# VectorE's reciprocals two tiles later and its division one tile later in the heads of a softmax attention

## Chip, cores and metric

One core of a Trainium2 chip runs one launch of the whole kernel. The metric is the device time in microseconds (us), lower is better. TensorE (PE) multiplies matrices, VectorE (DVE), ScalarE (ACT) and GpSimd (POOL) work on elements, and SyncE (SP) issues the transfers (DMA).

## What is computed

A block with a modulated layernorm, 16-head attention over 1024 tokens with a position bias, a gated residual, and then two layers of windowed attention with an MLP. The change lies in the first attention, for 2 batches x 16 heads = 32 heads:

```python
attn = jnp.einsum('bhqd,bhkd->bhqk', q, k) / math.sqrt(HD)
attn = attn + slopes[None, :, None, None] * rel[None, None, :, :]
attn = jax.nn.softmax(attn, axis=-1)
out = jnp.einsum('bhqk,bhkd->bhqd', attn, v)
```

## The kernel before

The kernel is written with one instruction stream for each engine and semaphores between them. The stage of the change is a loop over heads i = 0 to 31, and in each over tiles k = 0 to 7 of 128 keys (or, for the maxima, of 128 queries). Three heads are in work at a time:

- **Maxima of head i + 2.** TensorE writes a tile of raw scores (`max_step`, L836) into PSUM banks 4 and 5. VectorE adds the bias and takes the maximum of each row (`max_step`, L765: one long instruction and a short one that writes `M`). From head 2 on all tiles use the same two banks, so TensorE's scores of tile k + 1 wait until VectorE has written the maximum of tile k (`max_done`, L833). The eight maxima are turned by TensorE in the next head (`turn_m`, L842).
- **Scores, exponentials and products of head i.** TensorE writes scores with the maxima taken off (`qk_step`, L862), ScalarE takes exponentials into one of four buffers `E` (L738), TensorE multiplies them with the values (`pv_step`, L872). VectorE adds the exponentials of tiles 3, 5 and 7 (`sum_step`, L775: 3 + 5 behind the maximum of tile 5, and + 7 as the first thing of the next head), GpSimd those of the others and VectorE's sum (L684, L688).
- **Denominators and division of head i - 1.** In tile 2, TensorE sums GpSimd's result over partitions (`denominators`, L881), ScalarE copies it (`take_denominators`, L715), VectorE takes reciprocals in two halves (`invert`, L782), SyncE writes them to DRAM and reads them back spread over the partitions by two transfers (`spread_inverse`, L645 and L649), and VectorE multiplies the head's product by them (`divide`, L790, two instructions).

TensorE's order within a pair of tiles k, k + 1 (k even) is: scores k and k + 1, the maximum's scores of tile k, value products of tiles k - 1 and k, behind them in tile 2 the denominators and `turn_m`, then the maximum's scores of tile k + 1. Its value products of tile 0 of head i + 1 wait for the division of head i - 1 (L870), because they write the same bank.

SyncE's order in a head is: in every fourth head the keys and values of the next group (`load_kv`), queries (`load_qa`), the row of maxima (`load_m`), then `spread_inverse`.

In what follows "max 3" is the maximum of tile 3, on either engine as said. In the trace `XF` is the name under which the reciprocals and denominators stand, `xpos_sb` that of the sums, `junk` that of the maxima's discarded output.

Of the kernel before, what the change touches and what calls it, by code (L numbers as in the profile page):

```python
# [76 lines left out]
def need(eng, sem, count):  # L77

    if count > 0:
        eng.wait_ge(sem, count)  # L80
# [11 lines left out]
def adaln_block(nc, x, wq, wk, wv, wo, f_wqkv, f_qs, f_ks, f_wo, f_lg, f_lb, f_w1, f_b1, f_w2, f_b2,  # L92
# [7 lines left out]
    with ExitStack() as whole:  # L100
# [14 lines left out]
        def banks(a, n=1):  # L115
            return psum[:, a:a + n, :].rearrange("p b c -> p (b c)")
# [53 lines left out]
        with ExitStack() as ph:  # L170
# [63 lines left out]
            def need_landed(eng, b):  # L234

                for s in range(2):
                    eng.wait_ge(t_out[b][s], 48 * (TB // 2))
                    eng.wait_ge(v_out[b][s], 16 * (TB // 2))
# [308 lines left out]
        def residual(dve, t):  # L547

            s = t % 2
            need(dve, proj_done, t // 4 * 4 + 4 if t < TB else t + 1)  # L550
            dve.tensor_tensor(y[:, s, :], projected(t), rows[:, t // TB, ga, :], ALU.mult).then_inc(res_step, 1)
            dve.wait_ge(res_step, 4 * t + 1)
            dve.tensor_tensor(X[:, t, :], X[:, t, :], y[:, s, :], ALU.add).then_inc(res_step, 1)
            dve.wait_ge(res_step, 4 * t + 2)
            dve.bn_stats(bn[:, s, :], X[:, t, :]).then_inc(res_step, 1)
            dve.wait_ge(res_step, 4 * t + 3)
            dve.bn_aggr(mv[:, t, :], bn[:, s, :]).then_inc(res_step, 1)
# [22 lines left out]
        with ExitStack() as ph:  # L580
# [40 lines left out]
            def max_bank(i, k):  # L621

                return 4 if i >= 2 else (4, 0, 2)[(TB * i + k) % 3]
# [7 lines left out]
            with nc.Block() as block:  # L631
# [124 lines left out]
                @block.vector  # L756
                def _(dve):
                    def max_step(i, s, k):

                        need(dve, max_mm, TB * i + k + 1)  # L760
                        if k == 0:
                            need(dve, alibi_done, i + 1)
                            need(dve, m_turned, i - 1)
                        need(dve, max_done, TB * i + k)
                        dve.tensor_tensor_reduce(junk[:, :], banks(max_bank(i, k), 2), alibi[:, s, :], -1.0, BIG, ALU.add, ALU.min,  # L765
                                                 M[:, s, k:k + 1]).then_inc(max_done, 1)

                    def sum_step(i, s, n):
                        k = DVE_SUMS[n + 1]
                        need(dve, exp_done, TB * i + k + 1)  # L770
                        need(dve, sum_d_done, ND * i + n)
                        if n == 0:
                            need(dve, sum_p_done, NP * (i - 1))
                        first = E[:, DVE_SUMS[0] % 4, :] if n == 0 else sum_d[:, s, :]
                        dve.tensor_tensor(sum_d[:, s, :], first, E[:, k % 4, :], ALU.add).then_inc(sum_d_done, 1)  # L775

                    def invert(i, half):

                        need(dve, den_taken, i + 1)
                        need(dve, inv_out, 16 * i)  # L780
                        part = slice(half * DQ // 2, (half + 1) * DQ // 2)
                        dve.reciprocal(den_inv[:, part], den_sb[:, part]).then_inc(inv_done, 1)  # L782

                    def divide(i, ch):

                        need(dve, inv_in, 32 * (i + 1))
                        need(dve, pv_done, TB * (i + 1))
                        a, r = HD * ch, HD * (i % 2)
                        dst = OT[r:r + HD, i // H, (i % H) // 2, 4 * ch:4 * ch + 4, :].rearrange("p t c -> p (t c)")
                        dve.tensor_tensor(dst, banks(6 + i % 2)[a:a + HD, :], inv_wide[a:a + HD, :], ALU.mult)\  # L790
                            .then_inc(o_done, 1)

                    def head(i):
                        for k in range(TB):
                            if k == 0 and i > 0:
                                sum_step(i - 1, (i - 1) % 2, 1)
                            if i + 2 < HEADS:
                                max_step(i + 2, i % 2, k)
                            if k in (2, 3) and i > 0:
                                invert(i - 1, k - 2)  # L800
                            if k == 5:
                                sum_step(i, i % 2, 0)
                            if k == 6 and i > 0:
                                for ch in range(2):
                                    divide(i - 1, ch)

                    for i in range(2):
                        for k in range(TB):
                            max_step(i, i, k)
                    need_landed(dve, 1)  # L810
                    for i in range(HEADS):
                        head(i)
                    sum_step(HEADS - 1, (HEADS - 1) % 2, 1)

                    for half in range(2):
                        invert(HEADS - 1, half)
                    for t in range(EARLY):
                        residual(dve, t)
                    for ch in range(2):
                        divide(HEADS - 1, ch)  # L820
# [739 lines left out]
```

## Time and profile before

| | before |
|---|---|
| median of 3 runs | 1317.8 us (1313.16 to 1318.82) |
| the profiled execution's own time | 1316.46 us |
| its span, first to last instruction | 1314.7 us |
| TensorE busy in the span | 1115.1 us (85%) |
| VectorE busy | 1049.2 us (80%) |
| GpSimd busy | 849.0 us (65%) |
| ScalarE busy | 735.6 us (56%) |
| TensorE's granted clock, mean | 0.943 |

Busy time is the time in which an engine had an instruction in work; the span is a little shorter than the execution's own time, which has the start and end of the launch in it. The stage with the 32 heads lies between about 165 us and 800 us.

### The profile page before, as it was taken

The page shows a single profiled execution, that of the slowest core. Times are in us where ns is not written, and L with a number is a line of the kernel's source. Part 1 is how long each engine was busy: PE and PEld are TensorE (multiplying, and loading weights), DVE is VectorE, ACT ScalarE, POOL GpSimd, SP SyncE. Part 2 cuts the span into 40 slices and gives each one's busy share as a digit, 9 for nine tenths or more (in the row PEclk, how much of TensorE's full clock was granted, in tenths as well). Part 3 has the DMA queues.
Part 4 walks back from the last instruction along what each step waited for, and adds up shares of the span by engine and source line. Part 5 has one row for each costly group of instructions (what it writes and reads, how often), then busy time and mean ns, then how long its engine had stood idle before and what let it go on. Part 6 is the DMA issues. An engine that isn't in the chain of part 4 may idle for free. (4 is left out here: it accounts for less than half of the span.)

```text
span 1314.7 us, 23737 instructions
## 1 busy us (share of the span) xinstructions
PE 1115.1 (85%) x8256; PEld 692.6 (53%) x8256; DVE 1049.2 (80%) x2026; ACT 735.6 (56%) x1512; POOL 849.0 (65%) x488
## 2 busy tenths in 40 slices
PE   5776579999999999999999999467777896778788
PEld 3554535544455454555445548234555684455578
DVE  6898577777777777777777746599999589999957
ACT  3666625555555555555555551257676755777664
POOL 4556216566566666656656664698789249999916
PEclk9888769999999999999999999789898997999899
DMA  7567932142413314241331001000111100111111
GB/s 230 136 173 198 283 80 57 42 97 65 105 42 86 76 42 97 65 105 38 83 83 52 23 17 56 34 17 19 27 28 28 31 3 8 27 28 29 30 31 33
DMA packets 95237, 88.91 MB, mean 68 GB/s; under 512 B 22884, under 2 KB 74768, under 8 KB 95120
## 3 DMA queue, kind: packets, MB, share of 16 engines
q1 hardware_dynamic: 95120, 87.41, 26.2%
q8 instruction: 66, 1.08, 0.3%
q14 instruction: 51, 0.42, 0.1%
HBM read 53.57 MB, written 24.25 MB: 59 GB/s over the span
## 5 line engine op out<-in xcount | busy, mean ns | idle before, releaser
L738 ACT ACTIVATE E<-psum,keybias_sb 128x1024 f32<-128x1024 f32 x256 | 274.8, 1112 | 249.1 <-PE psum L862 235.9
L765 DVE CUSTOM_DVE_ANT_0 junk<-psum,alibi 128x1024 bf16<-128x1024 f32 x256 | 309.4, 1209 | 93.0 <-PE psum L836 80.2
L684 POOL TENSOR_TENSOR xpos_sb<-xpos_sb,E 128x1024 f32<-128x1024 f32 x96 | 231.2, 2408 | 130.7 <-ACT E L738 126.2
L872 PE MATMUL psum<-E,V 128*64 128x512 f32 x1024 | 248.0, 605 | 0.0
L836 PE MATMUL psum<-KH,QH 64*128 64x512 f32 x512 | 124.7, 481 | 20.9 <-DVE M L765 16.7
L688 POOL TENSOR_TENSOR xpos_sb<-xpos_sb 128x1024 f32<-128x1024 f32 x32 | 76.1, 2377 | 90.7 <-DVE xpos_sb L775 90.7
L1195 ACT ACTIVATE E_att<-S_att,nmax_att 128x128 f32<-128x128 f32 x256 | 99.0, 389 | 43.7 <-DVE nmax_att L1229 43.6
L1142 POOL TENSOR_TENSOR rinv_att<-ss_up_att,minus_half 128x16 f32<-128x16 f32 x32 | 120.8, 3775 | 2.7
L872 PEld LDWEIGHTS psum<-E,V 128*64 128x64 f32 x1024 | 62.1, 136 | 112.7 <-issue 105.7
L836 PEld LDWEIGHTS psum<-KH,QH 64*128 64x128 f32 x512 | 50.6, 191 | 124.1 <-DVE M L765 92.6
L782 DVE RECIPROCAL XF<-XF 128x128 f32<-128x128 f32 x64 | 60.4, 948 | 64.1 <-ACT XF L715 64.1
L862 PE MATMUL psum<-QH,KH 64*128 64x512 f32 x512 | 106.4, 406 | 3.4 <-ACT XF L715 1.0
L862 PE MATMUL psum<-QL,KH 64*128 64x512 f32 x512 | 103.4, 392 | 0.0
L862 PE MATMUL psum<-QH,KL 64*128 64x512 f32 x512 | 103.1, 391 | 0.0
L862 PE MATMUL psum<-QM,one_rows 64*128 64x512 f32 x512 | 103.0, 390 | 0.0
L1132 POOL TENSOR_TENSOR t_att<-raw_att,xpos_sb 128x1024 f32<-128x1024 f32 x32 | 100.5, 3142 | 0.0
L1323 PE MATMUL psum<-kT_att,qT_att 64*64 64x128 f32 x1024 | 42.4, 310 | 66.3 <-DVE nmax_att L1229 66.1
L684 POOL TENSOR_TENSOR xpos_sb<-E 128x1024 f32<-128x1024 f32 x32 | 76.4, 2388 | 30.0 <-ACT E L738 24.8
L1248 DVE TENSOR_TENSOR qk_att<-qk_att,rinv_att 128x1024 f32<-128x1024 f32 x32 | 90.3, 2823 | 5.8 <-POOL rinv_att L1142 4.7
L1323 PEld LDWEIGHTS psum<-kT_att,qT_att 64*64 64x64 f32 x1024 | 33.9, 152 | 88.6 <-issue 88.0
L1127 POOL TENSOR_TENSOR sq_att<-raw_att 128x1024 f32<-128x1024 f32 x32 | 66.6, 2083 | 14.1 <-ACT raw_att L1202 14.1
L1313 PE MATMUL psum<-fw_qkv,hT_att 128*128 128x512 f32 x128 | 66.1, 642 | 2.1 <-ACT raw_att L1202 2.1
(145 smaller groups left out, 2399.9 us busy)
## 6 DMA issues: line engine op xcount, KB each, us to landing
qa_scratch<-tT SPq DMA_DIRECT2D x32, 512.0 KB, 4.1
QH<-qa_scratch SPq DMA_DIRECT2D x64, 256.0 KB, 4.2
QL<-qa_scratch SPq DMA_DIRECT2D x64, 128.0 KB, 4.2
XF<-inverse_scratch SPq DMA_DIRECT2D x64, 128.0 KB, 2.9
vp_att<-v_att SPq DMA_DIRECT2D x64, 128.0 KB, 2.3
k_scratch<-tT SPq DMA_DIRECT2D x16, 256.0 KB, 4.6
KH<-k_scratch SPq DMA_DIRECT2D x16, 256.0 KB, 3.9
KL<-k_scratch SPq DMA_DIRECT2D x16, 256.0 KB, 5.1
```

The source lines that it names most:

```text
L684: pool.tensor_tensor(sum_p[:, s, :], first, E[:, k % 4, :], ALU.add)\
L688: pool.tensor_tensor(sum_p[:, s, :], sum_p[:, s, :], sum_d[:, s, :], ALU.add)\
L738: act.activation(E[:, k % 4, :], scores(k % 2), ACT.Exp, bias=kb).then_inc(exp_done, 1)
L765: dve.tensor_tensor_reduce(junk[:, :], banks(max_bank(i, k), 2), alibi[:, s, :], -1.0, BIG, ALU.add, ALU.min, M[:, s, k:k + 1]).then_inc(m ...
L836: last = pe.matmul(banks(max_bank(i, k) + ch), QH[rows, s, k * P:(k + 1) * P], KH[rows, g, ch * 512:(ch + 1) * 512], start=True, stop=True)
L862: last = pe.matmul(scores(k % 2)[:, ch * 512:(ch + 1) * 512], key[rows], query[rows, a:a + 512], start=(n == 0), stop=(n == len(terms) - 1))
L872: last = pe.matmul(banks(6 + i % 2)[HD * ch:HD * ch + HD, :], V[:, g, k, :], E[:, k % 4, ch * 512:(ch + 1) * 512], start=(k == 0), stop=(k ...
L1132: pool.tensor_tensor(t2[:, s].rearrange("p (q h) d -> p q h d", q=2), raw[:, s].rearrange("p (q h) d -> p q h d", q=2), sin, ALU.mult)\
L1142: pool.tensor_tensor(rinv[:, s, :], ss_up[:, s, :], minus_half[:, 0:NH], ALU.pow)\
L1195: act.activation(E[:, s, h, :], S[:, s, h, :], ACT.Exp, bias=nmax[:, s, h:h + 1], scale=-1.0, accum_out=den[:, s, h:h + 1]).then_inc(exp_d ...
L1248: dve.tensor_tensor(qk[:, s], qk[:, s], rinv[:, s, :][:, :, None].to_broadcast([P, NH, HD]), ALU.mult).then_inc(qk_done, 1)
L1323: last = pe.matmul(banks(5 + h % 2)[WIN * w:WIN * w + WIN, (h // 2) * P:(h // 2 + 1) * P], qT[a:a + HD, s, h // 2, WIN * w:WIN * w + WIN], ...
```

## The change

In heads with i > 0 VectorE's two reciprocals move from behind max 2 and max 3 to behind max 4 and max 5, and the division from behind max 6 to behind max 7. Nothing else is edited.

```diff
                             if i + 2 < HEADS:
                                 max_step(i + 2, i % 2, k)
-                            if k in (2, 3) and i > 0:
-                                invert(i - 1, k - 2)
+                            if k in (4, 5) and i > 0:
+                                invert(i - 1, k - 4)
                             if k == 5:
                                 sum_step(i, i % 2, 0)
-                            if k == 6 and i > 0:
+                            if k == 7 and i > 0:
                                 for ch in range(2):
                                     divide(i - 1, ch)
```

VectorE's row before, in head 1, from max 2 to the sum behind max 5 (each maximum is a row with `junk,M` and one with `M`):

```order
L765 ISA junk,M<-psum,alibi 128x1024
L765 ISA M 128x1
L782 RECIPROCAL XF<-XF 128x128
L765 ISA junk,M<-psum,alibi 128x1024
L765 ISA M 128x1
L782 RECIPROCAL XF<-XF 128x128
L765 ISA junk,M<-psum,alibi 128x1024
L765 ISA M 128x1
L765 ISA junk,M<-psum,alibi 128x1024
L765 ISA M 128x1
L775 TENSOR_TENSOR xpos_sb<-E 128x1024
```

The same stretch of the changed kernel, again from max 2 to the sum behind max 5:

```order
L765 ISA junk,M<-psum,alibi 128x1024
L765 ISA M 128x1
L765 ISA junk,M<-psum,alibi 128x1024
L765 ISA M 128x1
L765 ISA junk,M<-psum,alibi 128x1024
L765 ISA M 128x1
L782 RECIPROCAL XF<-XF 128x128
L765 ISA junk,M<-psum,alibi 128x1024
L765 ISA M 128x1
L782 RECIPROCAL XF<-XF 128x128
L775 TENSOR_TENSOR xpos_sb<-E 128x1024
```

The reciprocals now stand behind max 4 and max 5, and the second one is followed at once by the sum. Directly behind comes the second place, which before reads from max 6 through max 7 to max 0 of the next head:

```order
L765 ISA junk,M<-psum,alibi 128x1024
L765 ISA M 128x1
L790 TENSOR_TENSOR OT<-psum,XF 64x512 x2
L765 ISA junk,M<-psum,alibi 128x1024
L765 ISA M 128x1
L775 TENSOR_TENSOR xpos_sb<-xpos_sb,E 128x1024
L765 ISA junk,M<-psum,alibi 128x1024
L765 ISA M 128x1
```

And in the changed kernel it reads, from the same max 6 to the same max 0:

```order
L765 ISA junk,M<-psum,alibi 128x1024
L765 ISA M 128x1
L765 ISA junk,M<-psum,alibi 128x1024
L765 ISA M 128x1
L790 TENSOR_TENSOR OT<-psum,XF 64x512 x2
L775 TENSOR_TENSOR xpos_sb<-xpos_sb,E 128x1024
L765 ISA junk,M<-psum,alibi 128x1024
L765 ISA M 128x1
```

The division moved behind max 7 and is followed at once by the sum with which the next head begins. The rows of TensorE, ScalarE, GpSimd and SyncE are the same in both kernels. In heads 30 and 31 no maxima are left, and there VectorE's row is the same in both kernels too.

## Rows read from the trace of the kernel before

**Rows 1.** Busy time by stretch: start:end, length, busy (instructions) per engine, clock, DMA share, GB/s

```profile
212.65:751.37 538.72, 527.80 (x3392) 270.07 (x3389) 414.87 (x616) 284.44 (x308) 335.86 (x141) 1.00 0.28 69
...
164.00:175.00 11.00, 6.63 (x20) 2.40 (x16) 9.45 (x15) 2.67 (x5) 0.20 (x1) 0.50 0.20 55
```

**Rows 2.** Waits between 212.65 and 751.37 us: total, times, longest

```profile
PE psum L836 <- DVE M L765: 8.5, 15, 1.6
DVE OT L790 <- DMA XF<-inverse_scratch: 6.0, 7, 1.4
```

**Rows 3.** Timeline of TensorE, one head: start us, duration us, engine, line, what

```profile
521.87 0.51 PE L836 MATMUL psum<-KH,QH 64*128 64x512 f32 x2
...
524.35 0.47 PE L836 MATMUL psum<-KH,QH 64*128 64x512 f32 x2
...
526.61 0.50 PE L836 MATMUL psum<-KH,QH 64*128 64x512 f32 x2
...
530.97 0.51 PE L836 MATMUL psum<-KH,QH 64*128 64x512 f32 x2
...
532.71 0.40 PE L862 MATMUL psum<-QH,KL 64*128 64x512 f32 x2
532.94 0.39 PE L862 MATMUL psum<-QM,one_rows 64*128 64x512 f32 x2
533.39 0.49 PE L836 MATMUL psum<-KH,QH 64*128 64x512 f32 x2
...
535.69 0.50 PE L836 MATMUL psum<-KH,QH 64*128 64x512 f32 x2
...
540.82 0.50 PE L836 MATMUL psum<-KH,QH 64*128 64x512 f32 x2
```

**Rows 4.** Timeline of VectorE, the same head

```profile
522.22 0.95 DVE L782 RECIPROCAL XF<-XF 128x128 f32<-128x128 f32 x1 [1.64 <-ACT XF L715]
523.09 1.16 DVE L765 CUSTOM_DVE_ANT_0 junk<-psum,alibi 128x1024 bf16<-128x1024 f32 x1
...
524.18 0.95 DVE L782 RECIPROCAL XF<-XF 128x128 f32<-128x128 f32 x1
...
527.15 1.22 DVE L765 CUSTOM_DVE_ANT_0 junk<-psum,alibi 128x1024 bf16<-128x1024 f32 x1 [0.94 <-PE psum L836]
...
528.30 1.22 DVE L775 TENSOR_TENSOR xpos_sb<-E 128x1024 f32<-128x1024 f32 x1
529.44 1.22 DVE L765 CUSTOM_DVE_ANT_0 junk<-psum,alibi 128x1024 bf16<-128x1024 f32 x1
...
530.58 1.40 DVE L790 TENSOR_TENSOR OT<-psum,XF 64x512 f32<-64x512 f32 x2
532.01 1.23 DVE L765 CUSTOM_DVE_ANT_0 junk<-psum,alibi 128x1024 bf16<-128x1024 f32 x1
533.16 0.08 DVE L765 DVE_READ_ACCUMULATOR2_ANT M<- 128x1 f32 x1
```

**Rows 5.** Timeline of SyncE's transfer issues, the same head

```profile
525.15 0.51 SPq L645 DMA_DIRECT2D inverse_scratch<-XF  x1
526.77 1.14 SPq L649 DMA_DIRECT2D XF<-inverse_scratch  x2
```

**Rows 6.** The spreading transfers, all 64: us from issue to landing

```profile
DMA to landing us min/median/max: 2.8/2.9/4.0
```

**Rows 7.** Timeline of SyncE in a head that loads keys and values

```profile
504.64 0.52 SPq L645 DMA_DIRECT2D inverse_scratch<-XF  x1
507.60 1.14 SPq L649 DMA_DIRECT2D XF<-inverse_scratch  x2
```

**Rows 8.** Timeline of VectorE in that head

```profile
511.58 1.41 DVE L790 TENSOR_TENSOR OT<-psum,XF 64x512 f32<-64x512 f32 x2 [1.43 <-DMA XF<-inverse_scratch]
```

**Rows 9.** Timeline of ScalarE, exponentials of tile 7

```profile
529.64 1.11 ACT L738 ACTIVATE E<-psum,keybias_sb 128x1024 f32<-128x1024 f32 x1 [0.44 <-DVE xpos_sb L775]
```

**Rows 10.** Timeline of GpSimd, its last addition of a head

```profile
534.46 2.38 POOL L688 TENSOR_TENSOR xpos_sb<-xpos_sb 128x1024 f32<-128x1024 f32 x1 [2.71 <-DVE xpos_sb L775]
```

## Prediction, written before the changed kernel ran

> **What bounds the kernel now.** I first read the busy time of the stretch with the heads that the change touches, 28 heads from one `turn_m` to that of 28 heads later. TensorE is busy 527.80 of 538.72 us at the full clock, VectorE 414.87 [rows 1]. So the stage goes at TensorE's pace, and one head takes 538.72 / 28 = 19.24 us. The waits of the same stretch come next: TensorE stands 8.5 us for a maximum of VectorE, and VectorE 6.0 us for the spread reciprocals before the division [rows 2]. VectorE has a quarter of its time free, but TensorE can be only one maximum ahead of it, since all use one pair of banks. What decides is therefore where VectorE's extra work stands between two maxima, not how much there is of it.
>
> For that I laid the timelines of one quiet head side by side [rows 3, 4], with time 0 where TensorE starts the scores of max 3 (521.87). TensorE starts those of max 4 at 2.48, max 5 at 4.74, max 7 at 9.10, max 0 of the next head at 11.52, max 1 at 13.82 and the next max 3 at 18.95. The pairs of matmuls ahead of max 0 start 0.23 apart (532.71, 532.94), so it could have started at 533.17, which is 11.30; it did so 0.22 later, 0.15 behind the end of VectorE's max 7 (533.16 + 0.08). Without any wait a head is 18.73 us long. The difference to the mean, 0.51 x 28 = 14.3 us, is all that the best order for VectorE could give back in these heads.
>
> VectorE's durations, start to start so that the overlap of neighbours is counted once, are: a reciprocal 0.87 (522.22 to 523.09), a sum 1.14 (528.30 to 529.44), the division 1.43 (530.58 to 532.01), a maximum 1.15 (532.01 to 533.16), and 1.23 until its result stands. VectorE starts a maximum 0.54 behind TensorE's start (526.61 to 527.15) [rows 3, 4].
>
> **What the change removes.** The first reciprocal waits 1.64 us for ScalarE's copy of the denominators [rows 4]. Behind max 4 the copy has long been made and the wait goes, 28 x 1.64 = 46 us of VectorE. It is worth nothing to TensorE: max 3 comes earlier, but TensorE's max 4 starts at its own pace at 2.48 in either case.
>
> **What it moves, step by step.** Undisturbed, TensorE has 0.54 + 1.23 + 0.15 = 1.92 us of each interval of about 2.2 used up by VectorE, so only about 0.3 is free.
>
> Max 3 starts on VectorE at 0.54, max 4 at 3.02, and VectorE is free at 4.17. The first reciprocal reaches to 5.12, and max 5 would start at 5.28 anyway: it costs nothing. Max 5 leaves VectorE at 6.43. There the second reciprocal (ends 7.38), the sum (starts 7.30) and max 6 (starts 8.44) follow each other. Max 6 stands at 9.67, and TensorE's max 7, due at 9.10, starts at 9.82: **a wait of 0.72 us**.
>
> Max 7 starts on VectorE at 10.36, stands at 11.59, and VectorE is free at 11.51. TensorE's max 0 comes 2.20 behind max 7 (11.30 - 9.10), at 12.02, and waits for nothing. VectorE's max 0 however now has the division and a sum ahead of it. If the division could start at once, max 0 would start at 11.51 + 1.43 + 1.14 = 14.08, stand at 15.31, and TensorE's max 1 would start at 15.46 where 13.60 is due without waits (13.82 less the 0.22). **The order alone thus costs 1.86 us a head**, against the 0.51 of before.
>
> Third, **the division waits**. Between the second reciprocal and the division stood three maxima and a sum of room, now two maxima. The way through DRAM takes, from the end of the reciprocal (524.18 + 0.95), 0.02 to the issue of the write, 1.62 to that of the first read, 0.57 (half of 1.14) to that of the second [rows 5], and 2.9 to its landing [rows 6]: 5.11 us. From 7.38 the landing is at 12.49, and VectorE stands idle for 0.98 us from 11.51. Max 0 then starts at 12.49 + 1.43 + 1.14 = 15.06, stands at 16.29, and TensorE's max 1 starts at 16.44, 2.84 late. The rest, 5.13 us to the next max 3 (535.69 to 540.82 [rows 3]), has only light work for VectorE and is unchanged. A head becomes 18.73 + 2.84 = **21.57 us**, that is 2.33 more than 19.24.
>
> The Trainium skill, DMA: Bandwidth & Descriptors, Anatomy of one DMA, gives each transfer about 2.0 us plus its bytes at 436 GB/s (a fit for another issuing path). By it 4 KB and 128 KB in a row, with the same 0.59 of issues, would make an estimate of 4.9 us in place of 5.11, and the total about 6 us lower; the trace differs in the split (1.62 and 2.9) more than in the sum, and I go by the trace.
>
> What could hide or add to this: TensorE's value products of tile 0 wait for the division, which ends at 13.90; their turn comes at about 12.96 (max 0 and one group of products behind 12.02), but max 1 is later yet at 16.44, so this adds nothing. The exponentials of tile 7, which already waited 0.44 for the sum behind max 5 [rows 9], start at about 8.6 in place of 7.77 and end at 9.8, before the scores that need their bank at about 11. GpSimd's last addition, 2.38 us [rows 10], starts about 15.3 and is done at 17.7, 3 us before the denominators that stand ahead of the next max 3. SyncE issues the queries of a later head right behind the reads, a head before they are needed. The 7 waits of before for the transfers [rows 2] fall mostly in heads that load keys and values; there the write needed 2.96 us until the first read (504.64 to 507.60), and the division came 3.98 behind that [rows 7, 8]. The write now comes four microseconds later in the head, when those loads are through, so I give these heads the ordinary 5.11.
>
> **Sum.** 28 heads x 2.33 = 65.2. At the end of the last head with maxima the wait of 0.72 and the first value products' wait for the division (13.90 + 0.15 - 12.96 = 1.1) add 1.8, less the 0.2 of before: 1.6. Together 66.8 us, on 1316.46: 1383.3. The median of the runs lies 1.3 above that execution, so **1385 us**. The terms for 28 or 29 heads: pile-up before max 7, 20 us; pile-up before max 0 beyond that, 32 us; wait for the transfer, 28 us; less the 14.3 that are lost already.
>
> **Rivals.**
> - *As above, all three terms* (0.72). Its own range is 1372 to 1400: the landing at 2.8 to about 3.4, and some tenths of a microsecond a head on either side.
> - *No wait for the transfer*, only the order costs (0.07). 28 x (20.59 - 19.24) + 0.6 = 38.4, so 1356. For it: with DRAM and queue quiet the chain might be faster. Against: it would have to take 4.1 us from the reciprocal's end, where the fixed parts alone are 2.2 and no read landed under 2.8 [rows 5, 6].
> - *Slow transfers* (0.07). With the longest landing, 4.0 [rows 6], each head is 1.1 longer: 1417. If the chain took everywhere the 6.96 us of the head with loads (0.02 + 2.96 + 3.98 [rows 7, 8]) it would be 1.85 x 29 = 54 more: 1438. For it: the queries' loads now follow the reads at once.
> - *The clock* (0.05). The stage ran at 1.00, but at 0.50, the lower level of 1.2 GHz, where TensorE was busy 6.63 of 11 us before the heads [rows 1]. It will be busy about 18.7 of 21.6. Were the clock low in a tenth of the 600 us, at most half of those 60 us is lost: some 30 us more, 1415.
> - *No change* (0.04). The maxima are for two heads later, and if TensorE's own row let it go on with scores of the current head while VectorE is late, it would lose nothing: 1318. Against: max 1 stands in its row ahead of the next scores, and the 0.22 in the quiet head shows that it does wait.
> - *Faster* (0.05). VectorE's 46 us of waits for the denominators and the 6.0 for the transfers go, and if these were what made the maxima late, up to the 14.3 us come back: 1303. It needs VectorE's maxima 6 and 0 to be on time, so the blocks behind max 5 and max 7 would have to fit in some 0.3 us of room; they are 2.0 and 2.6 us long. It decides only if max 1 starts before 13.8.
>
> **How the numbers follow.** 1385 is the likeliest case. The range, 1364 to 1420, leaves out the cases at 1356, no change and faster (0.16) and the slowest chains, and takes in the bounds of the landing and a partly low clock. A measurement of this kernel can tell about 0.5% from no change. Slower by more than that: 0.72 + 0.07 + 0.07 + 0.05 = 0.91; within it 0.04; faster 0.05.
>
> **What would show it.** In the changed kernel's profile the reciprocals should have no wait for ScalarE, and the division one of about 1 us for the transfer in nearly all of the 29 heads. TensorE's scores of max 7 should start 5.1 us behind those of max 5 (4.4 before), and max 1 about 4.4 behind max 0 (2.3 before); a head should take 21.6 us, with TensorE about 87% busy and a granted clock of 1.00. I am wrong if the division starts right behind max 7, if max 1 isn't late, or if the clock falls.

## The result and the profile after

The changed kernel takes 1414.53 us in the median of 4 runs (1412.35 to 1418.58), before 1317.41 (1313.16 to 1318.82): a ratio of 1.0744, interval 1.0723 to 1.0764, that is 97 us more. The direction came as forecast, and so did the late max 1 and the wait of the division. The time lies in the range of 1364 to 1420, but 30 us above the 1385 that was called likeliest, and the granted clock fell, which the prediction had named as a sign of being wrong. The profiled execution took 1415.14 us, its span 1413.3.

The stretch of the same 28 heads as in [rows 1] comes first, then a run of quiet heads in it and a run of bad ones. The columns are those of [rows 1].

```profile
212.15:847.72 635.57, 551.02 (x3393) 282.39 (x3389) 425.00 (x616) 285.81 (x308) 357.42 (x141) 0.96 0.23 59
347.61:433.88 86.27, 75.66 (x488) 38.24 (x484) 60.72 (x88) 40.65 (x44) 51.10 (x21) 1.00 0.26 65
433.88:558.75 124.87, 105.36 (x610) 54.46 (x606) 75.89 (x110) 51.35 (x55) 65.06 (x26) 0.89 0.25 64
```

A head takes 635.57 / 28 = 22.70 us in place of 19.24. In the four quiet heads it is 86.27 / 4 = 21.57, just as forecast; in the five of the third row 124.87 / 5 = 24.97, with a mean granted clock of 0.89. The waits in the 28 heads, against [rows 2]:

```profile
PE psum L836 <- DVE M L765: 49.6, 56, 1.4
DVE OT L790 <- DMA XF<-inverse_scratch: 40.5, 28, 2.6
PE psum L872 <- DVE OT L790: 33.2, 28, 2.4
```

TensorE's waits for a maximum have gone from 8.5 us in 15 places to 49.6 in 56, two in each head; the division waits for its transfer in every head, 1.45 us in the mean, and TensorE's first value products wait for the division. ScalarE no longer holds up the reciprocals in these heads.

One quiet head on TensorE, which answers to [rows 3]. Max 3 is at 369.32; the following rows are max 7, max 0, one group of value products, the group that waits for the division, max 1 and the next max 3.

```profile
369.32 0.50 PE L836 MATMUL psum<-KH,QH 64*128 64x512 f32 x2
...
378.93 0.50 PE L836 MATMUL psum<-KH,QH 64*128 64x512 f32 x2 [0.45 <-DVE M L765]
381.10 0.40 PE L836 MATMUL psum<-KH,QH 64*128 64x512 f32 x2
381.43 1.08 PE L872 MATMUL psum<-E,V 128*64 128x512 f32 x4
383.32 1.08 PE L872 MATMUL psum<-E,V 128*64 128x512 f32 x4 [0.80 <-DVE OT L790]
385.75 0.50 PE L836 MATMUL psum<-KH,QH 64*128 64x512 f32 x2 [1.35 <-DVE M L765]
...
390.91 0.51 PE L836 MATMUL psum<-KH,QH 64*128 64x512 f32 x2
```

VectorE in the same head, which answers to [rows 4]: the second reciprocal, the sum, max 6, max 7, the division, the other sum and max 0.

```profile
375.71 0.95 DVE L782 RECIPROCAL XF<-XF 128x128 f32<-128x128 f32 x1
376.57 1.16 DVE L775 TENSOR_TENSOR xpos_sb<-E 128x1024 f32<-128x1024 f32 x1
377.65 1.21 DVE L765 CUSTOM_DVE_ANT_0 junk<-psum,alibi 128x1024 bf16<-128x1024 f32 x1
...
379.47 1.23 DVE L765 CUSTOM_DVE_ANT_0 junk<-psum,alibi 128x1024 bf16<-128x1024 f32 x1 [0.60 <-PE psum L836]
...
381.76 1.41 DVE L790 TENSOR_TENSOR OT<-psum,XF 64x512 f32<-64x512 f32 x2 [1.06 <-DMA XF<-inverse_scratch]
383.20 1.23 DVE L775 TENSOR_TENSOR xpos_sb<-xpos_sb,E 128x1024 f32<-128x1024 f32 x1
384.46 1.23 DVE L765 CUSTOM_DVE_ANT_0 junk<-psum,alibi 128x1024 bf16<-128x1024 f32 x1
```

Counted from max 3, the division starts at 12.44 (forecast 12.49), max 1 at 16.43 (16.44), the next max 3 at 21.59 (21.57). The signs that the prediction named are near but not exact: max 7 starts 4.92 us behind max 5 (374.01; forecast 5.1), and max 1 4.65 behind max 0 (4.4). The blocks behind max 5 and max 7 stand as the diff put them, and but for the wait of the division there is no room between their parts.

What the forecast lacks is in other heads. This is TensorE's timeline in one of the bad ones, at the same place: the group that waits for the division, max 1, and two of the eight pairs behind it.

```profile
524.45 1.08 PE L872 MATMUL psum<-E,V 128*64 128x512 f32 x4 [2.37 <-DVE OT L790]
526.88 0.79 PE L836 MATMUL psum<-KH,QH 64*128 64x512 f32 x2 [1.35 <-DVE M L765]
527.47 0.63 PE L862 MATMUL psum<-QH,KH 64*128 64x512 f32 x2
527.89 0.63 PE L862 MATMUL psum<-QL,KH 64*128 64x512 f32 x2
...
530.38 0.40 PE L836 MATMUL psum<-KH,QH 64*128 64x512 f32 x2
```

Two things differ. The wait for the division is 2.37 in place of 0.80 us, since the reciprocals landed later; and the pairs start 0.42 apart where [rows 3] have 0.23, so max 2 comes 3.50 us behind max 1 (2.19 in the quiet head). That is the lower clock of 1.2 GHz: between 527.40 and 529.50 us the granted clock is 0.50. Twelve of the 28 heads have such half-rate pairs behind max 1; five of them, in a row (434 to 558 us), have the long wait as well.

### The profile page after: what moved, and what is told of

It is laid out like the page before. It is cut to its first block and busy times, and to the rows that moved or that the text cites. A ratio compares the mean times of both kernels' runs of the same rounds, so it can differ in the third digit from the quotient of the medians.

```text
span 1413.3 us, 23737 instructions
## 1 busy us (share of the span) xinstructions
PE 1142.1 (81%) x8256; PEld 704.6 (50%) x8256; DVE 1060.0 (75%) x2026; ACT 737.0 (52%) x1512; POOL 871.9 (62%) x488
## 5 line engine op out<-in xcount | busy, mean ns | idle before, releaser
L765 DVE CUSTOM_DVE_ANT_0 junk<-psum,alibi 128x1024 bf16<-128x1024 f32 x256 | 313.2, 1223 | 192.7 <-PE psum L836 180.7
L684 POOL TENSOR_TENSOR xpos_sb<-xpos_sb,E 128x1024 f32<-128x1024 f32 x96 | 254.2, 2647 | 150.4 <-ACT E L738 145.8
L872 PE MATMUL psum<-E,V 128*64 128x512 f32 x1024 | 257.0, 612 | 34.2 <-DVE OT L790 34.2
L862 PE MATMUL psum<-QH,KH 64*128 64x512 f32 x512 | 111.7, 427 | 3.5 <-ACT XF L715 1.0
L862 PE MATMUL psum<-QL,KH 64*128 64x512 f32 x512 | 108.8, 413 | 0.0
L862 PE MATMUL psum<-QH,KL 64*128 64x512 f32 x512 | 108.0, 410 | 0.0
L862 PE MATMUL psum<-QM,one_rows 64*128 64x512 f32 x512 | 107.2, 407 | 0.0
L790 DVE TENSOR_TENSOR OT<-psum,XF 64x512 f32<-64x512 f32 x64 | 44.1, 689 | 44.2 <-DMA XF<-inverse_scratch 43.2
L782 DVE RECIPROCAL XF<-XF 128x128 f32<-128x128 f32 x64 | 60.3, 946 | 15.7 <-ACT XF L715 15.7
```

Source lines behind the costliest of these rows:

```text
L684: pool.tensor_tensor(sum_p[:, s, :], first, E[:, k % 4, :], ALU.add)\
L862: last = pe.matmul(scores(k % 2)[:, ch * 512:(ch + 1) * 512], key[rows], query[rows, a:a + 512], start=(n == 0), stop=(n == len(terms) - 1))
L872: last = pe.matmul(banks(6 + i % 2)[HD * ch:HD * ch + HD, :], V[:, g, k, :], E[:, k % 4, ch * 512:(ch + 1) * 512], start=(k == 0), stop=(k ...
```

## Experiments

Each was timed against the kernel before on the same chip. The period of a head, the waits and the clock are those of the same 28 heads in the profiled execution.

### One part of the change alone

First the reciprocals alone, with the division left behind max 6:

```diff
-                            if k == 7 and i > 0:
+                            if k == 6 and i > 0:
```

> Only the reciprocals are moved (behind max 4 and 5), the division stays behind max 6. Theory (order and transfer): the reciprocals land at 12.5 us of a head's time, so VectorE stands from 9.6 to 12.5 with max 7 queued behind it; max 7 stands at 15.15, TensorE starts max 0 at 15.3 and max 1 at 17.6, 4.0 us late. A head takes 22.7 us, the kernel about 98 us more than before, 1415, and more if the longer gap lowers the clock: ratio 1.075 to 1.10, no better than the whole change. Rival (the division's new place is what costs): it stays where it was, so the time should be within 10 us of before, ratio under 1.01.

Measured: 1475.91 us, ratio 1.121 (1.1177 to 1.1243), above the range of 1.075 to 1.10; a head takes 25.0 us. The rival is refuted: with the division in its old place the loss is larger, not smaller. The division starts where it was forecast, 12.37 us behind max 3 in this head (TensorE's row of max 3 first, then VectorE's division, then TensorE again):

```profile
361.39 0.51 PE L836 MATMUL psum<-KH,QH 64*128 64x512 f32 x2
...
371.00 0.50 PE L836 MATMUL psum<-KH,QH 64*128 64x512 f32 x2 [0.45 <-DVE M L765]
376.58 0.80 PE L836 MATMUL psum<-KH,QH 64*128 64x512 f32 x2 [3.23 <-DVE M L765]
377.31 3.08 PE L872 MATMUL psum<-E,V 128*64 128x512 f32 x8
380.31 0.50 PE L836 MATMUL psum<-KH,QH 64*128 64x512 f32 x2
```

```profile
373.76 1.41 DVE L790 TENSOR_TENSOR OT<-psum,XF 64x512 f32<-64x512 f32 x2 [2.81 <-DMA XF<-inverse_scratch]
```

Max 0 starts at 15.19, forecast 15.30. But I had not priced what follows: behind the gap of 3.23 us the two groups of value products take 3.08 us where 1.94 is usual, and max 1 comes at 18.92 instead of 17.6. The mean clock of these heads is 0.91, and it fell in each of the 28. The division's waits reach up to 4.4 us, but come to 89.1 us in all, 3.2 a head, where my expectation has 2.9. So later landings are worth some 8 of the 60 us above my 1415. The rest lies behind the gap, with the lower clock, and no run took it apart further.

Then the division alone, with the reciprocals left behind max 2 and 3:

```diff
-                            if k in (4, 5) and i > 0:
-                                invert(i - 1, k - 4)
+                            if k in (2, 3) and i > 0:
+                                invert(i - 1, k - 2)
```

> Only the division is moved (behind max 7), the reciprocals stay behind max 2 and 3. Theory: the reciprocals land at about 8.4, the division never waits; with the sum behind it max 0 is late and TensorE starts max 1 at 14.74 in place of 13.60. A head takes 19.9 us in place of 19.24: plus 18 us, 1335, ratio 1.010 to 1.017, clock at 1.00 in the stage. Rival (the division's new place is the cost): most of the 97 us appear here, ratio over 1.04.

Measured: 1338.77 us, ratio 1.0167 (1.014 to 1.0195), a head 19.98 us. The wait of the division is gone and TensorE has one wait of 1.2 to 1.35 us in each head, for max 0, with the clock at 1.00:

```profile
PE psum L836 <- DVE M L765: 35.7, 28, 1.3
```

The two parts do not add up: the first alone costs 160 us, the second 23, both together 97. Moved with the reciprocals, the division's step back lets max 7 pass before the wait for the landing.

### The changed kernel without the transfer

SyncE's `spread_inverse` is left out, with VectorE's wait for the write, and the division waits for one filling of its factors instead:

```diff
-                        if i > 0:
-                            spread_inverse(i - 1, (i - 1) % 2)
...
-                        need(dve, inv_in, 32 * (i + 1))
+                        dve.wait_ge(filled, 4)
```

> The changed kernel without the two-step transfer through DRAM: the division multiplies by constant ones, so the output lacks the softmax denominators; everything else, the reciprocals too, stays. Theory: the wait of the division (1.05 us in ordinary heads, up to 2.6) is gone, the order alone stays: a head takes 20.5 us, 1353, ratio 1.02 to 1.035, and no half-rate matmuls behind max 1. Rival (the order costs all, the transfer nothing): ratio stays near 1.074. Rival (the transfer is all): ratio within 0.5% of 1.

Measured: 1353.29 us, ratio 1.0272 (1.0241 to 1.0304), a head 20.47 us. That is the order's own cost, 37 us; the rest of the 97 hangs on the transfer. The clock stayed at 1.00, although TensorE still waits twice in each head:

```profile
213.13:786.42 573.29, 523.03 (x3393) 268.85 (x3389) 423.73 (x616) 284.30 (x308) 357.17 (x141) 1.00 0.22 52
```

```profile
PE psum L832 <- DVE M L762: 48.6, 56, 1.4
```

(L832 and L762 are the maximum's two lines in this kernel.) What is missing against the changed kernel is the wait for the division between max 0 and max 1.

### The gap filled with work

The changed kernel, with matmuls in the gap that weigh the exponentials with zeros:

```diff
+                        for n in range(extra):
+                            for ch in range(2):
+                                last = pe.matmul(banks(6 + i % 2)[HD * ch:HD * ch + HD, :], zeros[:, :],
+                                                 E[:, k % 4, ch * 512:(ch + 1) * 512], start=False,
+                                                 stop=(n == extra - 1))
                         last.then_inc(pv_done, 1)
```

> The changed kernel, with two more pairs of value products with zero weights behind the last tile of a head, which add nothing to the sums and lie in the gap in which TensorE waits for the division (about 1.9 us of matmuls). Theory (part of the loss is the clock, falling behind the gap of max 0 to max 1): the granted clock of the stage goes from 0.89 to 0.98 to nearly 1.00, no half-rate rows, ordinary heads stay at 21.6 us, and the kernel is some 15 to 20 us faster than the changed one, 1396, ratio 1.055 to 1.063. Rival (the clock's fall lies within the waits and costs nothing): the same 1.074 or slower.

Measured: 1397.58 us, ratio 1.0606 (1.0569 to 1.0644), some 16 us less than the changed kernel by doing more. The profiled execution is the fastest of the four, 1391.94 us; in it a head takes 21.89 us at clock 1.00, and not one of the 28 heads has half-rate pairs. The division waits 38.4 us in all, against 40.5 in the changed kernel, so the gain is not one of earlier landings. In order of time, max 0, the products of tile 7, the added matmuls, the products of tile 0, max 1 and max 2:

```profile
375.93 0.39 PE L837 MATMUL psum<-KH,QH 64*128 64x512 f32 x2
376.25 1.08 PE L876 MATMUL psum<-E,V 128*64 128x512 f32 x4
377.15 1.89 PE L881 MATMUL psum<-E,zeros_m 128*64 128x512 f32 x8
378.87 1.03 PE L876 MATMUL psum<-E,V 128*64 128x512 f32 x4
380.53 0.50 PE L837 MATMUL psum<-KH,QH 64*128 64x512 f32 x2 [0.63 <-DVE M L766]
382.71 0.39 PE L837 MATMUL psum<-KH,QH 64*128 64x512 f32 x2
```

The added 1.9 us of matmuls cost nothing, since TensorE only waits there, and max 2 comes 2.18 behind max 1. The rival, that the low clock hides within the waits, is refuted.

### The queries' loads out of the reads' way

```diff
-                            load_qa(sp, i + 3, (i + 3) % 4)
                         if i + 1 < HEADS:
                             load_m(i + 1, (i + 1) % 2)
+                        if i + 3 < HEADS:
+                            load_qa(sp, i + 3, (i + 3) % 4)
```

> The changed kernel, with SyncE's loads of the queries put behind the row of maxima, so that they are through before the reciprocals are written and do not follow the reads of the reciprocals. Theory (the long waits of 2.2 to 2.6 us in heads 13 to 17 come from the queries' transfers running into the reads): the division waits about 1.0 us in all heads, some 10 us less than the changed kernel, 1402 to 1406. Rival (those long waits are something else): the waits of over 2 us stay, ratio 1.074.

Measured: 1401.43 us, ratio 1.0624 (1.0601 to 1.0647), 13 us less than the changed kernel. (The bad heads that the expectation calls 13 to 17 are heads 11 to 15 of the program.) The division's waits fall from 40.5 to 30.4 us, and one of 28 is above 2 us, where there were five:

```profile
DVE OT L790 <- DMA XF<-inverse_scratch: 30.4, 28, 2.3
```

The waits thus account for 10 of the 13 us; half-rate pairs stand in 10 heads in place of 12. In the changed kernel the loads of the queries, 384 KB twice over, are issued 0.05 us behind the second read, as these rows of SyncE from the quiet head show:

```profile
378.31 1.14 SPq L649 DMA_DIRECT2D XF<-inverse_scratch  x2
379.50 0.59 SPq L157 DMA_DIRECT2D QH<-qa_scratch  x1
```

The intervals of the two kernels lie apart, so the place of the loads costs something. That they are the whole cause of the long waits is not shown: they follow the reads just as closely in the quiet heads (in the head at 369 us and in the bad one at 509), one long wait is left here, and the kernel with the filled gap has four heads in a row with them at another place (646 to 738 us).

### Both together

The last two edits in one kernel should bring back just what the prediction had left out.

> The changed kernel with both edits, the zero-weight products in the gap and the queries' loads behind the row of maxima. Theory (what the changed kernel loses beyond the 2.33 us a head that were predicted is the low clock and the long transfers, and nothing else): no half-rate rows, the division waits about 1.0 us in nearly all heads, every head takes about 21.5 us, the kernel 1382 to 1388, ratio 1.049 to 1.054. Rival (the two effects are one, long waits only making the clock fall): no better than the filled gap alone, ratio 1.060.

Measured: 1387.53 us (1387.06 to 1388.23), ratio 1.0531 (1.0513 to 1.0549), a head 21.65 us:

```profile
212.81:819.09 606.28, 571.97 (x3616) 285.40 (x3613) 424.96 (x616) 284.46 (x308) 357.43 (x141) 1.00 0.25 63
```

Each over its own runs of before, the changed kernel loses 97.1 us, with the gap filled 81.4, with the loads moved 84.1. Gains of 15.7 and 13.0 should leave 68.4; with both it loses 69.0. The intervals of these ratios reach 2 to 5 us to either side, so the agreement to 0.6 us is luck. But the interval lies below that of the filled gap alone, so the rival is refuted, and the two gains add up within the noise. What is left is within 3 us of the 66.8 of the prediction.

### The sum behind max 0

```diff
+                            if i + 2 < HEADS:
+                                max_step(i + 2, i % 2, k)
                             if k == 0 and i > 0:
                                 sum_step(i - 1, (i - 1) % 2, 1)
-                            if i + 2 < HEADS:
-                                max_step(i + 2, i % 2, k)
```

> The changed kernel, with the sum that opens a head put behind max 0 in place of ahead of it. Theory (max 0 is late by the pile of the wait, the division and this sum): max 1 starts 1.14 us earlier in each of 29 heads, some 33 us less, 1380, and fewer heads with a low clock. Rival (the transfer's wait alone sets the pace): no change against the changed kernel, 1414.

Measured: 1361.67 us, ratio 1.0327 (1.0311 to 1.0342), a head 20.84 us. The ordinary heads take 20.4 to 20.7, as 21.57 - 1.14 = 20.43 asks. The 19 us beyond my 1380 are for the most part the clock's. Only two of the 28 heads still have half-rate pairs, both with a division that waited over 2 us. The ten heads that lost them are worth some 16 us, as an estimate: a head with such pairs takes 23.16 us in the changed kernel (280.89 to 304.05 us) where the quiet head ahead of it, with the same wait of the division within 0.02, takes 21.57. The division's waits, 34.6 us in place of 40.5, give another 6. That is 22 us, which is what the two profiled executions have beyond the 32 of the order (1415.14 - 1361.36 = 54). So a gap cut by 1.1 us saved more than 1.1 us.

### One piece to a gap

From the kernel before, not from the changed one. The sum moves behind max 0 as above, and the division is split:

```diff
-                            if k == 6 and i > 0:
-                                for ch in range(2):
-                                    divide(i - 1, ch)
+                            if k in (6, 7) and i > 0:
+                                divide(i - 1, k - 6)
```

> The kernel before, with VectorE's extra work laid one piece to a gap between maxima: reciprocals behind max 2 and 3 as before, the sum behind max 5, the halves of the division behind max 6 and max 7, the other sum behind max 0. Theory: a gap has room for about 1.35 us, so no piece makes TensorE wait except in the heads where the reciprocals land late; a head goes from 19.24 to 18.8, 1305, ratio 0.988 to 0.994. Rival (the order of before leaves nothing to gain, its waits come from elsewhere): ratio 0.998 to 1.002.

Measured: 1305.19 us, ratio 0.9902 (0.9887 to 0.9916), a head 18.84 us. The rival, that the order of before leaves nothing, is refuted. Heads without a late landing take 18.62 to 18.67. VectorE from max 6 to max 0: each maximum has at most one piece behind it.

```profile
524.08 1.22 DVE L765 CUSTOM_DVE_ANT_0 junk<-psum,alibi 128x1024 bf16<-128x1024 f32 x1
...
525.23 0.68 DVE L790 TENSOR_TENSOR OT<-psum,XF 64x512 f32<-64x512 f32 x1
526.16 1.23 DVE L765 CUSTOM_DVE_ANT_0 junk<-psum,alibi 128x1024 bf16<-128x1024 f32 x1 [0.26 <-PE psum L835]
...
527.42 0.69 DVE L790 TENSOR_TENSOR OT<-psum,XF 64x512 f32<-64x512 f32 x1
528.26 1.23 DVE L765 CUSTOM_DVE_ANT_0 junk<-psum,alibi 128x1024 bf16<-128x1024 f32 x1
...
529.40 1.22 DVE L775 TENSOR_TENSOR xpos_sb<-xpos_sb,E 128x1024 f32<-128x1024 f32 x1
```

### And the keys and values behind the reciprocals

In the last kernel `load_kv` moves in SyncE's order, with its waits:

```diff
-                        if i % GROUP == 0 and i // GROUP + 1 < HEADS // GROUP:
...
-                            load_kv(sp, i // GROUP + 1, (i // GROUP + 1) % 2)
...
                             spread_inverse(i - 1, (i - 1) % 2)
+                        if i % GROUP == 0 and i // GROUP + 1 < HEADS // GROUP:
...
+                            load_kv(sp, i // GROUP + 1, (i // GROUP + 1) % 2)
```

> The kernel with one piece to a gap, and in every fourth head the loads of keys and values issued behind the transfer of the reciprocals in place of ahead of it. Theory (the 5 to 6 us left in 6 of its heads, 19.2 to 19.9 in place of 18.65, come from the write of the reciprocals queueing with those loads): they go, 1300, ratio to before 0.985 to 0.989. Rival (the loads now crowd the reads, which land later, or the next head's queries): the same or slower, 0.990 or more.

Measured: 1301.2 us, ratio 0.9873 (0.9851 to 0.9895). The interval overlaps that of the kernel before it (0.9887 to 0.9916), so the times alone do not show the step between the two; the traces do. A head takes 18.65 us, and the division's waits fall from 7.9 to 1.8 us in the 28 heads:

```profile
DVE OT L790 <- DMA XF<-inverse_scratch: 1.8, 4, 0.6
```

The profile shows no matmul that waits for a maximum any more; TensorE is busy 520.45 of 522.17 us.

## Why the prediction came close, and where it was short

- **The bound** was read rightly: what counted was the place of VectorE's work between two maxima, not its amount. The 46 us of waits that the change took from VectorE brought nothing that shows: one piece to a gap keeps them and is faster than before.
- **The order's cost.** Forecast 38.4 us for the kernel without the transfer's wait, measured 37.1 with the transfer left out.
- **The wait before max 7** was put at 0.72 us; it is 0.51 (max 7 at 9.61 in place of 9.82, [rows 3] having 9.10), since the second reciprocal started 0.04 earlier than forecast, the sum and the maximum behind it 1.08 apart (376.57 to 377.65) and not 1.14, and TensorE 1.28 behind that maximum's start (377.65 to 378.93) and not 1.38. It made little difference to the head. VectorE was free for the division 0.13 earlier, the landing came only 0.05 earlier, and the division waited 1.06 us in place of 0.98. That max 1 then met the forecast to 0.01 us is luck: max 0 started on VectorE 0.08 late (15.14, not 15.06), and TensorE followed it 1.29 later, not 1.38.
- **The division's wait** of 0.98 us a head holds in the ordinary heads. Its price of 28 us shows as 69.0 - 37.1 = 32 us, with two long landings still in it.
- **The step that failed** is "SyncE issues the queries of a later head right behind the reads, a head before they are needed", priced at nothing. They are early enough themselves, but the reads ahead of them land later: 1.45 us of wait in the mean against 0.98. With the loads moved, 13 us come back, though why only some heads have the long landings stays open. I had put this among the rivals at 0.07, as a case instead of the likeliest one; it was an addition to it.
- **The term that was missing** is the clock, which I took as 1.00, with a rival at 0.05 and 30 us. By my own last line I was wrong if it fell, and it did, in 12 of 28 heads. It is worth about 16 us by the filled gap. I argued from the mean busy share, about 87%; what the clock fell behind was the run of waits between max 0 and max 1.
- **The sum** of 66.8 us was 97. The order and the ordinary wait come to 69 (1387.53 - 1318.56), and the other 28 are these two. The rivals at 1415 (clock) and 1417 (slow transfers) come close to the measured 1414.53 by luck, since each put on one cause about what the two cost together. The range held, 5 us below its upper end, because both had been let into it.
- **Faster and no change** were rightly low, but the room was misread. The 0.3 us is what TensorE can spare in an interval; VectorE's own room behind a maximum is 2.2 - 1.15 + 0.3 = 1.35 us, since it would otherwise wait for the next scores. In the last two experiments pieces of up to 1.14 us fit there without a wait. The blocks of the change, 2.0 and 2.6 us, fit in neither figure.
- **What the best order could give back** was put at 14.3 us, from a head of 18.73 us without waits. The heads of the last two kernels without a late landing take 18.62 to 18.67, so it is some 16 to 17 us; the last kernel gains 17.

## What to carry to other kernels

Where one engine may be only one step ahead of another, lay the other's extra work one piece to a gap, and count a gap's room from one start to the next; moving a piece away from a wait can cost more than the wait did. Put a consumer of a transfer behind enough work to cover the whole chain from its producer, and look what is issued right behind that transfer. When you price a new wait on TensorE, add what the clock may do behind it, and take that from rows with gaps like it, not from the mean busy share.

## What the hardware showed that was not expected

The clock fell to 1.2 GHz in 12 of 28 heads of the changed kernel, and the length of the waits does not sort them. In all 28 TensorE waits for the division and, behind one group of products of 1.0 us, for max 1. The second wait is 1.35 us in all but one head, where it is 0.46 because the products between them already ran at half rate. The first wait was 2.0 to 2.4 us in five of the twelve and 0.8 to 1.6 in the other seven, and 0.7 to 1.5 in the sixteen in which the clock stayed at 2.4 GHz. With the queries' loads moved the clock fell in ten heads with a first wait of 0.7 to 1.0 us, and stayed up in the one in which it was 2.0. What decides between them stays open.

Without the wait for the division (the kernel without the transfer, and the division alone) the clock never fell in the 28 heads of either, whose longest wait is 1.35 us. Behind one wait of 3.2 us or more (the reciprocals alone) it fell in all 28. With matmuls of zero weights in the gap it stayed up in all 28, in both kernels that have them.
